# The four-expert mixture of a decoder: all experts for all tokens, or sorted blocks of 128 slots

## What is computed

```python
tid = jnp.clip(token_ids, 0, VOCAB - 1)              # VOCAB = 12500, ids are 13 to 99985
expert_ids = jnp.minimum(tid // tokens_per_expert, E - 1)   # E = 4
out = jnp.zeros_like(hidden_states)
for e in range(E):
    g = jax.nn.silu(jnp.einsum('bsd,fd->bsf', hidden_states, Wg[e]))
    u = jnp.einsum('bsd,fd->bsf', hidden_states, Wu[e])
    y = jnp.einsum('bsf,df->bsd', g * u, Wd[e])
    out = jnp.where((expert_ids == e)[..., None], y, out)
```

## Time and profile before

| | |
|---|---|
| time, median of 3 runs | 430.35 us |
| lowest and highest of them | 426.91 and 431.69 us |
| span of the profiled execution | 429.5 us |
| PE busy | 413.5 us (96% of the span) |
| POOL, DVE, ACT busy | 270.6, 255.2, 241.6 us |

### The profile page before, as it was taken

The page is one execution under the profiler, slowest core; times in us unless marked ns, Lnnn a source line. Parts: engine busy times, 40 slices in busy tenths (PEclk is TensorE's granted clock), DMA queues, the critical chain, the costliest instruction groups (busy, mean ns, idle before and its releaser), DMA issues.

```text
span 429.5 us, 9350 instructions
## 1 busy us (share of the span) xinstructions
PE 413.5 (96%) x3645; PEld 361.4 (84%) x3645; DVE 255.2 (59%) x637; ACT 241.6 (56%) x423; POOL 270.6 (63%) x237
## 2 busy tenths in 40 slices
PE   8999999999999999899999999999699999999994
PEld 7888999988889888788888899798578989888983
DVE  4778657748536338966654588655455676343243
ACT  4848654764484775352734767573526757554543
POOL 1744454564798577674876548457647386877763
PEclk9999999999999999999999999999999999999998
DMA  8644000021233313042222103121523332565402
GB/s 256 195 149 145 3 2 0 2 76 50 73 91 123 103 53 124 24 127 96 79 86 76 38 0 111 51 88 63 167 74 96 118 103 78 151 165 151 141 33 98
DMA packets 19623, 39.29 MB, mean 91 GB/s; under 512 B 2763, under 2 KB 7371, under 8 KB 19580
## 3 DMA queue, kind: packets, MB, share of 16 engines
q1 hardware_dynamic: 19004, 38.17, 28.8%
q10 hardware_dynamic: 576, 0.53, 0.4%
HBM read 37.08 MB, written 1.08 MB: 89 GB/s over the span
## 4 chain that ended last, share of the span: by engine, by line
PE 75%; DVE 10%; issue 4%; ACT 4%; DMA 3%; SPq 2%; POOL 1%; POOLq 0%; DVEq 0%; ACTq 0%
PE bank L492 13%; PE bank L493 13%; PE bank L495 13%; PE bank L762 8%; PE bank L764 7%; PE bank L763 7%; PE bank L842 2%; DMA pk_raw<-w_attn_dram 2%; PE bank L781 2%; PE bank L830 1%; DVE q_buf L1584 1%; DMA brow<-cw_dram 1%; PE bank L515 1%; PE bank L812 1%; PE bank L813 1%
## 5 line engine op out<-in xcount | busy, mean ns | idle before, releaser
L1307 POOL TENSOR_TENSOR h_lo<-hraw,h_hi 128x512 fp32r<-128x512 f32 x76 | 98.1, 1294 | 77.3 <-ACT h_hi L1097 77.2
L492 PE MATMUL bank<-xT_hi,pk_hi 128*128 128x512 f32 x256 | 102.9, 402 | 1.1 <-DVE hraw L1625 1.1
L493 PE MATMUL bank<-xT_hi,pk_lo 128*128 128x512 f32 x256 | 101.0, 395 | 0.0
L1097 ACT ACTIVATE h_hi<-hraw 128x512 fp32r<-128x512 f32 x76 | 47.8, 629 | 72.3 <-DVE hraw L1625 70.3
L1625 DVE TENSOR_TENSOR hraw<-bank,sil 128x512 f32<-128x512 f32 x76 | 52.4, 689 | 54.6 <-ACT sil L1085 24.6
L495 PE MATMUL bank<-xT_lo,pk_hi 128*128 128x512 f32 x256 | 80.4, 395 | 0.0
L762 PE MATMUL bank<-pk_hi,h_hi 128*128 128x256 f32 x272 | 77.8, 286 | 0.2 <-issue 0.2
L764 PE MATMUL bank<-pk_hi,h_lo 128*128 128x256 f32 x272 | 76.9, 283 | 0.0
L763 PE MATMUL bank<-pk_lo,h_hi 128*128 128x256 f32 x272 | 76.8, 282 | 0.0
L1313 POOL TENSOR_TENSOR pk_lo<-pk_raw,pk_hi 128x512 fp32r<-128x512 f32 (+1 forms) x44 | 74.8, 1700 | 2.8 <-ACT pk_hi L1115 2.6
L492 PEld LDWEIGHTS bank<-xT_hi,pk_hi 128*128 128x128 f32 x256 | 48.2, 188 | 11.8 <-DVE hraw L1625 1.6
(11 more groups left out here) (256 smaller groups left out, 736.6 us busy)
## 6 DMA issues: line engine op xcount, KB each, us to landing
pk_raw<-pk_f_dram SPq DMA_DIRECT2D x28, 384.0 KB, 3.3
pk_raw<-pk_f_dram SPq DMA_DIRECT2D x16, 512.0 KB, 3.5
pk_raw<-pk_f_dram SPq DMA_DIRECT2D x16, 256.0 KB, 3.3
kv_buf<-pk_x_dram SPq DMA_DIRECT2D x4, 512.0 KB, 3.7
x_tok<-x_rows_dram SPq DMA_DIRECT2D x1, 1024.0 KB, 9.5
pk_raw<-pk_x_dram SPq DMA_DIRECT2D x4, 256.0 KB, 6.2
brow<-cw_dram SPq DMA_DIRECT2D x4, 256.0 KB, 3.4
cw_late<-cw_dram SPq DMA_DIRECT2D x4, 256.0 KB, 4.0
```

The source lines that it names most:

```text
L492: pe.matmul(o, w(kc)[0], x(kc)[0], start=kc == 0, stop=False)
L493: pe.matmul(o, w(kc)[1], x(kc)[0], start=False, stop=False)
L1097: A(h_hi[:, row, at * 512:(at + 1) * 512], hraw[:, s % 2, :], ACT.Copy).then_inc(sems["hid_hi"], 1)
L1307: pool.tensor_tensor(h_lo[:, row, q], hraw[:, s % 2, :], h_hi[:, row, q].bitcast(F32), ALU.subtract).then_inc(sems["hid_lo"], 1)
```

## The change

Each half's tokens are sorted by expert into at most NB = 7 blocks of 128 slots, each block with one expert; 14 blocks in all, whatever the ids are. Unused slots are zeros.

1. Routing moves to the start. `k0` (DVE) makes `route0`, then PE counts with 8 small matmuls against a triangle and a square of ones (`x0_rank`, between `b0.1` and `b0.2`), and `k1` to `k3` on DVE (18 small instructions) turn the counts into a slot for each token (`slot_i`) and a weight offset for each block (`block_w`).
2. SP fills the scratch arrays `xs_dram` with zeros (two DMAs of 0.9 MB).
3. `P<h>` (POOL): after the norm, 4 indirect DMAs write the 4 token tiles to their slots in `xs_dram`. `L<h>` (SP) reads the 7 blocks back (2 DMAs).
4. `x<h>.<stage><block>`: stage 0 transposes a block (2 transposes) and splits it, stage 1 is the gate (6 matmuls of 256 columns, weights addressed by a register), silu and product, stage 2 transposes the hidden block (2) and splits it, stage 3 is the down product (6 matmuls of 256) and an ACT copy to `y_sent`.
5. `Y<J>` (SP) stores each block to `ys_dram`. `Q<h>` (POOL) gathers the rows back with 4 indirect DMAs once all 7 blocks are stored, and `x<h>.40` to `x<h>.43` (DVE) add them to `x_tok` and begin the statistics.
6. `n0.2` and `n1.2` are gone. The golden layer starts when all blocks are through. All four experts' split weights now lie in `xp_hi` and `xp_lo`.

The orders around it, cut:

```diff
 PE_ORDER
-... b1.7 n0.2 b1.8 g0 g1 b1.9 g2 g3 d0 ... g13 r0.2 g14 d5 r0.3 g15 g16 u16 d6 g17 u17 d7 g18 ...
+b0.0 b0.1 k0 b0.2 ... b1.7 b1.8 b1.9 x0.00 x0.01
+x0.10 x0.02 x0.11 x0.03 x0.12 x0.20 x0.04 x0.13 x0.21 x0.30 x0.05 x0.14 x0.22 x0.31 x0.06 x0.15 x0.23 x0.32 x0.16
+x0.24 x0.33 x0.25 x0.34 x1.00 x0.26 x0.35 x1.01 x1.10 x0.36 x1.02 x1.11 x1.20 x1.03 x1.12 x1.21 x1.30 x1.04 x1.13
+x1.22 x1.31 x1.05 x1.14 x1.23 x1.32 x1.06 x1.15 x1.24 x1.33 x1.16 x1.25 x1.34 x1.26 x1.35 x1.36 r0.2 g0 g1 u0 r0.3 u1
+g2 u2 g3 d0 u3 g4 u4 ...
 ACT_ORDER
+... G0 D0 n0.1 b1.8 G1 D1 n1.1 x0.00 x0.01 x0.10 x0.02 ... x1.35 r0.1 x1.36 r0.2 r0.3 s0 h0 s1 G2 h1 r0.4 s2 D2 ...
 POOL_ORDER
+... X0 X1 X2 X3 n0.0 P0 G0 D0 n1.0 P1 G1 D1 Q0 r0.0 Q1 l0 G2 l1 D2 G3 l2 ...
 DVE_ORDER
+k0 p2 b0.0 b0.1 k1 ... b0.7 k2 b1.1 b0.8 k3 p5 b1.2 n0.0 ... b1.8 n1.0 x0.00 x0.01 x0.10 ...
+x1.22 x1.05 x1.14 x1.23 x1.06 x0.40 x1.15 x1.24 x0.41 x1.16 x0.42 x1.25 x0.43 x1.26 r0.0 r0.2 r0.3 r0.4 m0 m1 r0.5 m2
+a0 m3 m4 x1.40 x1.41 x1.42 x1.43 r1.0 ...
 SP_ORDER
+G0 D0 G1 D1 S0 L0 G2 D2 L1 Y0 Y1 ... Y13 G3 D3 ...
```

New functions (DVE's `x0_routes` holds the lines that made `route0` before):

```diff
+            def x0_load(h):                                            # SP
+                if h:
+                    sp.wait_ge(sems["x0_t_ps"], 3)
+                sp.wait_ge(sems[f"x0_sent{h}"], 16 * HT)
+                rows = xs_dram[h][:, :].rearrange("(j p) d -> p j d", p=P)
+                to = x_sent[h][:, 0:NB * D].rearrange("p (j d) -> p j d", d=D)
+                sp.dma_start(to[:, 0:2, :], rows[:, 0:2, :]).then_inc(sems["x0_in0"], 16)
+                sp.dma_start(to[:, 2:NB, :], rows[:, 2:NB, :]).then_inc(sems["x0_in1"], 16)
+            def x0_store(J):                                           # SP
+                sp.wait_ge(sems["x0_y"], J + 1)
+                sp.dma_start(ys_dram[h][j * P:(j + 1) * P, :], y_sent[h][:, j * D:(j + 1) * D]
+                             ).then_inc(sems[f"x0_ys{h}"], 16)
+            def x0_send(h):                                            # POOL
+                pool.wait_ge(sems["x0_zero"], 32)
+                pool.wait_ge(sems["slots_ready"], 1)
+                for t in range(HT):
+                    pool.wait_ge(sems["ln_done"], 4 * nth(h) + t + 1)
+                    pool.indirect_dma_start(xs_dram[h][:, :], bass.IndirectOffsetOnAxis(ap=slot_i[:, T:T + 1], axis=0),
+                                            x_tok[:, T, :], None).then_inc(sems[f"x0_sent{h}"], 16)
+            def x0_fetch(h):                                           # POOL
+                pool.wait_ge(sems[f"x0_ys{h}"], 16 * NB)
+                if h:
+                    pool.wait_ge(sems["x0_added"], HT)
+                for t in range(HT):
+                    pool.indirect_dma_start(o_tok[:, t, :], None, ys_dram[h][:, :],
+                                            bass.IndirectOffsetOnAxis(ap=slot_i[:, T:T + 1], axis=0)
+                                            ).then_inc(sems[f"x0_got{t // 2}"], 16)
+            def x0_expert(h, i):                                       # PE, stage 1 of 0 to 3
+                    if j == 0:
+                        pe.wait_ge(sems["slots_ready"], 2)
+                        for k in range(J, J + NB):
+                            block_at[k] = pe.value_load(block_w[0:1, k:k + 1], min_val=0, max_val=(EX - 1) * W_X0)
+                    pe.wait_ge(sems["x0_xh"], J + 1)
+                    for c in range(KC):
+                        w = bass.ds(at + c * D, D)
+                        pe.matmul(o, xh[:, c, :], ew_hi[:, w], start=c == 0, stop=False)
+                        pe.matmul(o, xh[:, c, :], ew_lo[:, w], start=False, stop=False)
+                    pe.wait_ge(sems["x0_xl"], J + 1)
+                    for c in range(KC):
+                        m = pe.matmul(o, xl[:, c, :], ew_hi[:, bass.ds(at + c * D, D)], start=False, stop=c == KC - 1)
+            def x0_expert(h, i):                                       # DVE
+                if stage == 0:   # xT_lo = transposed block - xT_hi
+                elif stage == 1: # hraw = gate * silu(gate)
+                elif stage == 2: # h_lo = transposed hidden - h_hi
+                else:
+                    dve.wait_ge(sems[f"x0_got{t // 2}"], 32 * (h + 1))
+                    TT(x_tok[:, T, :], x_tok[:, T, :], o_tok[:, t, :], ALU.add).then_inc(sems["x0_added"], 1)
+                    dve.wait_ge(sems["x0_added"], T + 1)
+                    link(dve.bn_stats(stats[:, t, :], x_tok[:, T, :]))
```

More of the change, by code:

```diff
@@ L678, in _, with x0_rank @@
                 pe.matmul(bank[3][:, :], zero_r[:, 0:P], zero_r[:, :], start=True, stop=True)
+            def x0_rank():
+                pe.wait_ge(sems["rank_in"], 2)
+                per_tile = route0[:, :, :].rearrange("p (h t) e -> p h t e", h=2)
+                ranks = bank[1][:, 0:TILES * EX].rearrange("p (h t e) -> p h t e", h=2, t=HT)
+                counts = bank[1][:, TILES * EX:(TILES + 2) * EX].rearrange("p (h e) -> p h e", h=2)
+                pe.matmul(ranks, tri_m, per_tile, start=True, stop=False, skip_group_check=True)
+                for t in range(1, HT):
+                    pe.matmul(ranks[:, :, t:HT, :], ones_m, per_tile[:, :, 0:HT - t, :], start=False, stop=t == HT - 1,
+                              skip_group_check=True)
+                for t in range(HT):
+                    m = pe.matmul(counts, ones_m, per_tile[:, :, t, :], start=t == 0, stop=t == HT - 1,
+                                  skip_group_check=True)
+                m.then_inc(sems["rank_ps"], 1)
@@ L951, in beside @@
                     first(i, h)
-                elif step[0] == "n":
-                    if i == 2:
-                        transposes(h)
+                elif step[0] == "x":
+                    x0_expert(h, i)
                 elif step[0] == "r":
@@ L964, in _ @@
                     beside(step)
+                elif step[0] == "k":
+                    x0_rank()
                 elif step[0] == "g":
@@ L1906, in _ @@
                     prepare(i)
+                elif step[0] == "k":
+                    if i:
+                        x0_slots(i)
+                    else:
+                        x0_routes()
                 else:
```

369 lines of the change are left out of this document (255 added, 114 removed).

## The result

The changed kernel takes 447.4 us (median of 4 runs, 446.59 to 448.94) against 430.4: a ratio of 1.041, 95% interval 1.0361 to 1.0458, or 17.0 us more. The forecast was 439 (its sum was 8.9 us more), in a range of 428 to 453. The direction was right and the range holds the time, but the size is half of what was measured.

A forecast was written before the change was run, and what follows sets the result against it. PE was taken to bound the kernel (busy 413.5 of 429.5 us). Uncovered waits and slow clock move the golden layer's mark from 91.6 to 100.5, 8.9 more: span 438.4, plus 0.85 to the median, 439 us; range 428 to 453.

The forecast's parts named there:

- k0 at 0.9 us: In the startup: the 8 counting matmuls on PE ahead of attention's queries, with no idle time there, cost 0.9 us.
- the waits nobody covers: Before, between and behind the blocks: hand-overs with nothing over them cost more than the 20 us of matmuls saved.
- Block period, indirect DMA on POOL, address registers: Mixture: 1.85 us per block at PE's pace; 1.3 us of POOL per indirect DMA; register-addressed matmuls at no extra.
- b1.9 ends at 44.9: Last matmul of half 1's projection on PE, before the blocks: ends at 44.9 us, against 45.9 before the change.
- Register loads at 1.0: PE: half 0's seven loads fall in idle time; half 1's seven cost 1.0 us, bounds nothing to 3.0.
- The seventh block's y at 73.5: Half 0's last block: ACT's copy of its output, which releases the gather, ends at 73.5 us.
- a fill of 1.3: At the first block: filling the pipe of blocks costs 1.3 us, for the first split and silu's table load.
- The clock falls at 2.8 each: First blocks and golden start: after idle time PE runs at 1.2 GHz, costing 2.8 us each time.
- The charge of 8.9 for the golden start: Start of the golden layer: r0.3 1.7 us, waits for silu, d0 and copies 4.4, slow clock 2.8.
- The gather: Half 0, after its blocks: row pairs land at 80.4 and 83.0 us, DVE waits, first golden gate at 91.6.
- From there on ... PE bounds them as before: After the golden layer's start: work, orders and loads are unchanged, so the 8.9 us of delay stays the same.
- slow register addresses: Rival, block matmuls: each register-addressed one costs 0.24 us, not 0.12, so 1.4 more per block, 453 us; chance 0.2.

## Why the prediction had the direction right and half the size

The step that failed is the price of the register loads: the sum had 1.0 us for half 1's seven, hidden in part behind queued matmuls, and the runs show 4.1 us of idle PE and 5.4 with the half clock behind it. The next is the start, k0 at 0.9 us, where half 0's norm came 4.0 later.

- **That the waits nobody covers outweigh 20 us of matmuls**: right. Each place was named: ahead of the first block, between the last block and the golden layer, d0 and silu at its start.
- **Block period, indirect DMA on POOL, address registers**: right (1.87 for 1.85, 1.26 for 1.3, no extra).
- **k0 at 0.9 us**: 4.0 in the profile. It has 16 matmul passes and not 8 (1.7 us by the trace; the run without counting gives 1.4), the half clock in this execution goes with another 1.5, and 1.0 is left, probably the late x columns.
- **b1.9 ends at 44.9**: 50.2. 3.1 of the miss is the start. The transposes of half 0's norm and the gate steps g0 and g1, which used to stand in the waits ahead of it, are gone; PE is at half clock in b1.9 in this profile and in six of the eleven others of changed kernels, and its 24 matmuls take 4.6 us and not 2.9. The forecast looked for clock falls only behind the longest idle times. On the first block it costs 0.7 us, by the pair of runs with and without it; more is hidden behind half 0's register loads, which the forecast had in idle time and which end last as soon as b1.9 is fast.
- **Register loads at 1.0**: this is the step that failed most. The hole of half 1's is 4.1 us, over the upper bound of 3.0, and another fall of the clock comes behind it; 5.4 together by the run with fixed addresses. The reason given, that matmuls queued ahead would cover them, was wrong: nothing ran on PE during the 4.1 us.
- **The seventh block's y at 73.5**: 78.4, 21.4 us after the first gate, just as in the forecast. That is luck. The loads are in it at 4.1 and not 1.0; against that the forecast counted ten gates where the list has eight (1.4 us), took a fill of 1.3 that does not show (PE is busy for 3.00 of 3.00 us from 57 to 60), and charged 2.8 for the clock where 0.8 at most is seen.
- **The clock falls at 2.8 each**: they are there, but cost 0.8 at most at the first block: half clock was priced as if PE set the pace. At the first golden gates 1.8 are seen up to the router, and the rest is open. The charge of 8.9 for the golden start is the measured one (15.2 - 6.2 us of lateness at the first gate = 9.0). Of its parts, the wait for silu took 1.4 as charged and the one of d0 2.1, not 2.8; the others were not shown one by one, so the match of the sum may be luck.
- **The gather**: 18.1 us from y to the first golden gate (the forecast's own list of what the saving is spent on has 16, and adds up to 26 us, not to 28.9), 19.4 measured. It landed later than forecast but nobody waited, because DVE was still with the blocks. With the loads moved the forecast wait is there, at 0.35 us.
- **"From there on ... PE bounds them as before"**: held to 214.9 us to the tenth. Then 2.4 us more appeared in holes of instruction issue, whose places follow from the length of PE's list. The kernel before has them too, and it gains 3.7 us from 11 matmuls of zeros. The pairs of kernels with the same startup differ by 15.1 us (30 short ones added) and 20.3 (20 of 256 columns), the originals by 17.0. Up to the scores their profiles differ by 14.1, 16.2 and 15.2. So the change itself costs 14 to 16 us, and 1 to 4 more come behind the scores, where holes change place and size with the list.
- **The rivals**: the forecast's step of slow register addresses was the way to 453, and its mechanism did not happen. What took the time there was the loading of the registers, which the forecast had in the sum at a fifth of its cost.

In sum: at the first golden gate the forecast was 6.2 us short: 3.1 for the start, 1.8 from there to the first block, 4.4 for the loads and the clock behind them and 1.3 from y to the gate, less 4.4 for the wrong count, the fill and the overcharged clock (1.4, 1.3 and 2.0 by themselves). The later holes added 2.4.

## What to carry to other kernels

Cost a register load on PE like a stall of the whole engine: several us for a set, wherever it stands, so put it where PE is idle anyway. When work is taken out of a full engine, look at what that work had covered, the short waits too, and price the slower clock only where this engine is the last one. When one wait is removed, ask which one ends next: with b1.9 fast it was the register loads. And before a difference of 1% between two kernels is explained by the edit, look for holes in instruction issue far from it: they can move with any edit that changes the length of the list.

## What the runs showed of the hardware

- Seven `value_load`s on PE from the on-chip memory took 4.0 to 4.2 us ahead of half 1's blocks and 3.9 ahead of half 0's (no counting), fourteen 6.0 to 7.0, with PE idle throughout.
- PE's 128 matmuls of 32 rows by 17 columns take 1.26 us; holes of 0.2 to 2.7 us in instruction issue occur in such groups, the smaller ones at places that move one for one with the number of matmuls ahead. PE can be at 1.2 GHz behind one (matmuls of 512 columns 0.42 apart from 234.7 to 237.3, behind 1.98 us), or not (clock 1.00 behind 2.53 us).
- A matmul of 8 columns took as long as one of 256: 0.12 from start to start for 30 of them, 0.21 for 39 at the kernel's start. Matmuls of 256 columns lie 0.21 apart up to 7.2 us with nine of 512 columns ahead of them, up to 11.4 with 20 of 8 columns and up to 13.9 with 39.
- A VectorE operation of 8 columns (0.15 to 0.17 us alone) took 1.26 to 2.27 us when it met a GpSimd operation, and one of 32 columns (0.19 alone) 1.28 and 2.21.
- SP went on 1.5 us after POOL's part of the last indirect scatter of 128 rows; a gather pair had landed 3.9 us after POOL's part.
